# A message pass whose step is written as edge products, message products, node sums, with its gathers paced by the edge products

## The reference

```python
def _mlp(h, W, b, gamma, beta):
    h = jax.nn.relu(h @ W + b)
    mu = jnp.mean(h, axis=0)
    var = jnp.mean(jnp.square(h - mu), axis=0)
    return gamma * (h - mu) * jax.lax.rsqrt(var + EPS) + beta

node_feat = _mlp(x, W_node, b_node, g_node, beta_node)
edge_feat = _mlp(edge_attr, W_edge, b_edge, g_edge, beta_edge)
row, col = edge_index[0], edge_index[1]
message = jnp.concatenate([x[row], x[col], edge_feat], axis=1)
message = _mlp(message, W_msg, b_msg, g_msg, beta_msg)
agg = jax.ops.segment_sum(message, col, num_segments=node_feat.shape[0])
return agg + node_feat
```

## Time and profile before

| | us |
|---|---|
| median of three runs (11304.01 to 11315.23) | 11309.91 |
| the profiled execution: its own time | 11304.11 |
| the profiled execution: its span | 11302.3 |
| of it before the message pass | 482 |
| of it in the message pass, 482 to 3361 | 2879 |
| of it behind the message pass (attention and norms) | 7941 |

### The profile page before, as it was taken

One profiled execution on the slowest core, in us unless ns is written; L12 is line 12 of the kernel. 1 busy time (PEld: TensorE's weight loads), 2 busy tenths in 40 slices (PEclk: granted clock), 3 DMA queues, 4 the chain that ended last, 5 costly groups with the idle time before them and its releaser, 6 DMA issues. The chain is left out here.

```text
span 11302.3 us, 137890 instructions
## 1 busy us (share of the span) xinstructions
PE 6476.3 (57%) x31155; PEld 5674.4 (50%) x31155; DVE 4578.9 (41%) x11750; ACT 3536.6 (31%) x7293; POOL 6608.7 (58%) x6483
## 2 busy tenths in 40 slices
PE   4866666666665555555556555555556555555555
PEld 2355555555554444444446444444446444444445
DVE  5744444444443333333333333333333333333334
ACT  2611111111113333333332333333332333333332
POOL 0166666666645666666663666666663666666663
PEclk8555555555555666666665666666665666666665
DMA  6111111111112111111111111111111111111111
GB/s 119 33 32 32 32 32 32 32 32 32 32 25 34 34 35 34 34 34 34 34 34 26 34 34 35 34 34 35 34 34 25 35 34 34 35 34 34 34 34 25
DMA packets 339638, 395.84 MB, mean 35 GB/s; under 512 B 225961, under 2 KB 233503, under 8 KB 337399
## 3 DMA queue, kind: packets, MB, share of 16 engines
q0 software_dynamic: 206976, 330.75, 15.2%
q1 hardware_dynamic: 132615, 64.61, 3.0%
HBM read 368.10 MB, written 26.82 MB: 35 GB/s over the span
## 5 line engine op out<-in xcount | busy, mean ns | idle before, releaser
L764 POOL DMA_INDIRECT rows<-table_a,idx x4851 | 4786.3, 987 | 2692.3 <-issue 1579.1
L1346 PE MATMUL ps<-ident,work 128*128 128x128 f32 x4872 | 1187.9, 419 | 2583.7 <-issue 2446.6
L764 POOL DMA_INDIRECT rows<-table_m,idx x1617 | 1764.9, 1091 | 1081.0 <-PE ps L1002 556.2
L1363 PE MATMUL ps<-rows,work 128*128 x9744 | 1777.3, 353 | 954.4 <-ACT work L1295 852.7
L1346 PEld LDWEIGHTS ps<-ident,work 128*128 128x128 f32 x4872 | 935.2, 220 | 2677.9 <-issue 2534.4
L1363 PEld LDWEIGHTS ps<-rows,work 128*128 128x128 f32 x9744 | 1645.8, 262 | 1151.5 <-issue 1149.3
L1302 ACT ACTIVATE work<-work,small 128x896 f32<-128x896 f32 x696 | 724.9, 1042 | 3609.0 <-issue 2234.7
L1239 DVE SCALAR_TENSOR_TENSOR work<-dstf,big,select 128x224 f32 x696 | 314.4, 452 | 3157.1 <-SPq L707 1710.4
L1228 DVE CUSTOM_DVE_ANT_0 work<-work,ps 128x896 f32<-128x896 f32 x696 | 757.0, 1088 | 1234.8 <-issue 944.0
L1354 PE MATMUL ps<-ident,work 128*128 128x128 f32 x4872 | 1120.7, 403 | 84.1 <-DVE work L1249 51.3
L1002 PE MATMUL ps<-work 128*97 128x32 f32 x3248 | 577.4, 350 | 896.8 <-DVE work L928 892.9
(11 more groups left out here) (252 smaller groups left out, 6314.9 us busy)
## 6 DMA issues: line engine op xcount, KB each, us to landing
rows<-table_a,idx POOLq DMA_INDIRECT x4851
rows<-table_m,idx POOLq DMA_INDIRECT x1617
big<-edge_parts SPq DMA_DIRECT2D x231, 45.5 KB
edge_parts<-big SPq DMA_DIRECT2D x6, 1617.0 KB, 7.6
work<-edge_parts SPq DMA_DIRECT2D x50, 192.0 KB
table_a<-work SPq DMA_DIRECT2D x3, 2474.5 KB, 22.6
b_dram<-big SPq DMA_DIRECT2D x3, 1176.0 KB, 8.1
big<-b_dram SPq DMA_DIRECT2D x3, 1176.0 KB, 18.3
```

What stands on the lines that cost most here:

```text
L764: pool.indirect_dma_start(rows[:, k % RING, j, 0:width], None, table, bass.IndirectOffsetOnAxis(ap=idx[:, k // CHUNK, at:at + 1], axis=0)) ...
L1346: last = pe.transpose(ps[:, 4 + j // 4, (j % 4) * P:(j % 4 + 1) * P], prob[:, par, j, :], ident[:])
L1363: last = pe.matmul(ps[:, 6 + par, 0:D + 1], probT[:, par, j, :], rows_of(at("slot", 3))[:, j, 0:D + 1], start=(j == 0), stop=(j == TPG - 1))
```

## The change

TensorE's iteration becomes `edge_product`(q), `message_product`(q-1), `node_sums`(q-2). VectorE's becomes `match_turned`(q) (L901, L896, L908 of before), `add_source`(q-1), `add_squares`(q-2), `accumulate`(q-2), `match`(q) (L891, L906 of before). ScalarE's iteration stays. The gathers of group g wait for `u_ready` at g, the edge products of step g-1, in place of `s_ready` at g-2. At the start, the gathers of groups 0, 1 and 2 went without that wait; now only those of group 0 do. The attention layers' lead is 1, for which `max(lead, 0)` is the same number.

```diff
-LEAD_M = 2
+LEAD_M = 0
...
-                        if not (isinstance(g, int) and g <= emit.lead):
+                        if not (isinstance(g, int) and g <= max(emit.lead, 0)):
                             pool.wait_ge(emit.steps_told, g - emit.lead)
...
-            steps_told, lead = step_sems["s_ready"], LEAD_M
+            steps_told, lead = step_sems["u_ready"], LEAD_M
...
+                def match_turned(q, par, at):
+
                     dve.wait_ge(s["dst_ready"], q + 1)
                     if not (isinstance(q, int) and q < 2):
                         dve.wait_ge(s["pre_ready"], 2 * q - 2)
...
+                    if not (isinstance(q, int) and q == 0):
+                        dve.wait_ge(s["win_ready"], q)
+                    dve.tensor_scalar(b_low, b_all[:, bass.ds(at("parts", 0) + ROW_B, D)],
+                                      selects[0:3 * WA, bass.ds(at("table", 0) + WA + 1, 1)], None, ALU.mult).then_inc(s["low_ready"], 1)
                     dve.wait_ge(s["low_ready"], q + 1)
                     dve.scalar_tensor_tensor(b_win[:, par], b_all[:, bass.ds(at("parts", 0), D)],
                                              selects[0:3 * WA, bass.ds(at("table", 0) + WA, 1)], b_low,
                                              ALU.mult, ALU.add).then_inc(s["win_ready"], 1)
+
+                def match(q, par, at):
+
+                    d = dstf[:, bass.ds(at("ready", 0), TPG)]
+                    dve.scalar_tensor_tensor(eq[:, par], d.unsqueeze(2).broadcast_to([P, TPG, WA]), base_w[:, bass.ds(at("window", 0), 1)],
+                                             iota[:, bass.ds(at("shift", 0), WA)].unsqueeze(1).broadcast_to([P, TPG, WA]),
+                                             ALU.subtract, ALU.is_equal).then_inc(s["eq_ready"], 1)
+                    dve.wait_ge(s["eq_ready"], q + 1)
+                    dve.tensor_reduce(inside[:, par], eq[:, par], AX.X, ALU.add).then_inc(s["inside_ready"], 1)
...
                 def step(q, par, live, at):
+                    if live(0):
+                        match_turned(q, par, at)
+                    if live(1):
+                        add_source(q - 1, (par - 1) % 2, at)
+                    if live(2):
+                        add_squares(q - 2, (par - 2) % 2, at)
                     if live(2):
                         accumulate(q - 2, (par - 2) % 2, at)
                     if live(0):
                         match(q, par, at)
-                    if live(2):
-                        add_squares(q - 2, (par - 2) % 2, at)
-                    if live(1):
-                        add_source(q - 1, (par - 1) % 2, at)
                 return step
...
                 def step(q, par, live, at):
+                    if live(0):
+                        edge_product(q, par, at)
+                    if live(1):
+                        message_product(q - 1, (par - 1) % 2, at)
                     if live(2):
                         node_sums(q - 2, (par - 2) % 2, at)
-                    if live(1):
-                        message_product(q - 1, (par - 1) % 2, at)
-                    if live(0):
-                        edge_product(q, par, at)
                 return step
```

More of the change, by code:

```diff
@@ L904, in match @@
                                       ALU.subtract, ALU.is_equal).then_inc(s["eqt_ready"], 1)
-                    dve.wait_ge(s["eq_ready"], q + 1)
-                    dve.tensor_reduce(inside[:, par], eq[:, par], AX.X, ALU.add).then_inc(s["inside_ready"], 1)
+                    if not (isinstance(q, int) and q == 0):
+                        dve.wait_ge(s["win_ready"], q)
+                    dve.tensor_scalar(b_low, b_all[:, bass.ds(at("parts", 0) + ROW_B, D)],
+                                      selects[0:3 * WA, bass.ds(at("table", 0) + WA + 1, 1)], None, ALU.mult).then_inc(s["low_ready"], 1)
                     dve.wait_ge(s["low_ready"], q + 1)
```

## The result

The changed kernel takes 10938.9 us (median of four runs, 10938.1 to 10940.1), the kernel before 11310.9 us (median of four, run beside it): a ratio of 0.967, 95% interval 0.966 to 0.969. That is 3.3% less, inside the range and 187 us above the 10752 us predicted.

A forecast was written before the change was run, and what follows sets the result against it. No engine was full; a 12.26 us loop of TensorE and VectorE waits set the step. 518.1 + 230 x 9.9 + 1.85 + 6.2 = 2803 for the pass's end, 558 us less, gave 10752 us; range 10590 to 10960.

The forecast's parts named there:

- The ring and its cut: Message pass: waits between TensorE and VectorE form a loop of 12.26 us a step; the new order cuts it.
- The pace of the gathers doesn't bind: Message pass: the gathers' new wait closes a loop of 15.1 us for three groups, 5.0 us a group.
- A step is 9.9 us, and all of it is POOL: Message pass: GpSimd's seven gathers set the new step, 8.75 us plus 1.15 of holding by VectorE.
- the holding: Message pass: VectorE instructions L901, L886 and L928 delay gathers that start in them, 1.15 us a step.
- L901 holds up a gather that starts in it: Message pass, new order: the fifth gather sits in L901, is let go at 6.47 and ends at 7.41 us.
- that rival: Message pass, gathers held less: step 8.9 to 9.4 us; at 9.1, 10568 us; chance 0.17.
- the prediction's own signs: Message pass: wrong if POOL idles 2 us or more a group, L901 holds no gather, or PE's 8.4 us grows to the step.
- held more, or a small wait on top: Message pass: DVE burst, slower landing or SyncE falling behind; step 10.8 us, 10959 us; chance 0.15.
- The start: Before the first edge product: 21 early gathers shrink to 7; gain at most some 10 us, taken as 0.
- Sign and chance: Whole kernel: faster 0.94, same 0.02, slower 0.04.
- The slow rival, one group in flight: Message pass: edge product g+1 waits for gather g's landing; 15.1 us a step, 11954 us; chance 0.04.

The follow-up runs named there:

- order_only: Changed kernel with the old gather pace (wait for node sums of step g-3), on a chip where the kernel before takes 10001 us: 9285.7 us, ratio 0.928.
- pace_only: Kernel before, old order, with the new gather pace (wait for edge products of step g-1), same chip where it takes 10001 us: 9999.7 us, ratio 0.9998.
- lead_m1: Changed kernel with gathers of group g held until the edge products of step g, one step later: 10877.3 us beside 10889.7 us for the changed kernel.
- order_again: Changed kernel with the old gather pace, on a chip where the kernel before takes 11295 us: 10942.9 us, ratio 0.969.
- burst: Kernel before with a lead of 7, so 56 gathers go out at once at the start, where the kernel before takes 11280 us: 11332.7 us (one run).

## Why the prediction came out as it did

**The ring and its cut: right.** The old chain was the bound; the new order took it away, by itself (order_only, pace_only), and what is left on TensorE is 8.37 us against the 8.38 summed. The register loads of the step lists, which I had not counted, stand in the trace and cost nothing where TensorE is full.

**The pace of the gathers doesn't bind: right for the time.** A step later (lead_m1) or the old pace (order_again) changes under 0.2%. In the trace of the slow kind GpSimd does stop at the pace after its runs, but only because the signal is late.

**"A step is 9.9 us, and all of it is POOL": wrong in its size, twice, in opposite directions.** The pass of the changed kernel has 2492 us from its first edge product (500.40) to its end (2992.59), 10.79 us a group.

First, the holding. GpSimd's gathers have a mean of 0.999 us (I expected 1.11) and 0.30 between them, 7 x 1.30 = 9.1 us a group, not 9.9. The step that failed is "L901 holds up a gather that starts in it", carried over to the new order. In order_only a gather starts 0.27 us into L893, the same instruction, and takes its 0.94; one that starts in L931 takes 1.61.

```profile
2012.87 1.21 DVE L893 TENSOR_SCALAR work<-ps,base_w,select 96x896 bf16<-96x896 f32 x1
2019.31 0.86 DVE L931 SCALAR_TENSOR_TENSOR work<-work,small 128x672 f32<-128x672 f32 x1
```

```profile
2013.14 0.94 POOL L764 DMA_INDIRECT rows<-table_m,idx  x1 [0.30 <-issue]
2018.13 0.94 POOL L764 DMA_INDIRECT rows<-table_m,idx  x1 [0.31 <-issue]
2019.38 1.61 POOL L764 DMA_INDIRECT rows<-table_m,idx  x1 [0.30 <-issue]
```

L931 ends at 2020.17, and 2019.38 + 1.61 is 0.94 behind 2020.05. Over the whole pass none of the gathers that start inside L893 is held, 221 in order_only and 209 in the changed kernel. The rule of the Trainium skill (GPSIMD Engine Reference, Key points) names two SBUF inputs, which L931 has and L893, with its PSUM input, has not. The new order's traces agree with it, and the step of 9.1 us that I worked out for that rival is what GpSimd's own rows now give. The old order's trace doesn't agree: there L901 held 206 of 228. Worth (9.1 - 9.9) x 231, some -187 us.

Second, the late signals, which no part of the prediction had: 10.79 - 9.1 = 1.7 us a group, some 390 us. This term is what is left, so the sum closes by itself: with 15 us gained at the start (500.40 in place of 515.53), -187 + 390 - 15 = 188, and the time was missed by 187. What bears the term out is one and the same kernel on both kinds of chip: 9.24 us a group in order_only, 10.77 in order_again, 1.53 more.

That the time fell inside the range is luck. With the holding and the start alone it would have been 10752 - 187 - 15 = 10550, below 10590; with the late signals and the start alone 10752 + 390 - 15 = 11127, above 10960. By the prediction's own signs it was wrong twice: L901 (L893) holds no gather, and GpSimd stands 2.8 us for "remote" in about every second group. The rival "held more, or a small wait on top", 10959 us, had the place and the size, with another cause. One of its three causes is there, SyncE falling behind, but in the step shown `landed` still came 7.8 us ahead of the signal that L922 waited for.

**The start.** I gave at most 10 us to fewer gathers ahead; it was 15, and burst shows the cause: it is the same lateness. On the fast kind 21 gathers at once cost nothing: the first edge product comes at 504.27 with 21 (order_only) and at 504.13 with 7 (pace_only).

**Sign and chance: right.** The slow rival, one group in flight, was never near.

**What stays open.** The changed kernel itself never met the fast kind of chip; order_only's 0.928 there, and the equality of the two paces elsewhere, argue for some 9280 us, but that wasn't measured. What differs between the chips isn't known, nor by what way GpSimd's gathers delay TensorE's signals. All times come from recorded executions, so whether the signals are as late when nothing is recorded can't be told. And what holds a gather in L901 wasn't tried. In the old order the 206 gathers that start 0.43 us or more into it are held to some 0.13 us before its end, and the 22 that start 0.14 to 0.23 us into it are free. But where a gather starts can't be all of it: in order_only 64 gathers start 0.4 to 0.7 us into the same instruction, and all are free.

## What to carry to other kernels

Where no engine is full, find the ring of waits, and put first in each engine's turn the part whose inputs are oldest; then each engine's own sum is the next bound. Here it came out within 0.1 us on the fast kind of chip (8.38 summed for 8.37 on TensorE, 9.18 for 9.24 on GpSimd). A follower that becomes the bound runs without rests for the first time: look in the trace for a stretch where it already did (here the 21 gathers at the start, and the attention layers' pauses after fourteen), since what it does to the others shows there. A hold read from one order isn't a mechanism: L901 held nearly every gather in the old order and none in the new. Where a page names a cause and one instruction doesn't fit it, give the page's case more of the chance (it had 0.17 together with another phase).

## What the hardware showed unexpectedly

In three of four sets of runs, gathers issued by GpSimd without a rest made TensorE's signals late, and no other engine's of those that compute. Beside a run of 14 gathers, 17 us, they came 7.5 to 11.2 us behind their matmuls (15.5 us at most in the pass); in a run of 56, 70 us, one came 19.1 us behind. A rest of 3.4 us after every seven gathers removed it, and one of 0.69 us didn't. On the chip of the fourth set gathers without a rest cost nothing, and the same kernel before took 10001 us in place of 11280 to 11311.
